# Score matmuls of two attentions issued for two heads at a time, PSUM rings of four and four, another step order

## What is computed

```python
x = x + tanh(g_xattn[0]) * _L0_xattn_ref(ctx_2048, _layernorm(x), mask, mask, ...)
x = x + tanh(g_ffn[0])   * _L0_ffn_ref(_layernorm(x), ...)
x = x + tanh(g_xattn[1]) * _L1_xattn_ref(_layernorm(x), ctx_2048, ...)
x = x + tanh(g_ffn[1])   * _L1_ffn_ref(_layernorm(x), ...)
# _L0_xattn_ref: 8 heads of 16; softmax(q k / 4, masked keys -inf) v, then W_out on [tgt, update]
# _L0_ffn_ref: dist = softmax(mean(x @ Wr + br)); idx = sorted top 4 of 16 heads, per batch
#              softmax(Qs Ks / 8) Vs for these heads, then Wo
# _L1_ffn_ref: top 2 of 8 experts per token: silu(xs w1 + b1) w2 + b2, times (xs w3 + b3); plus shared
```

## Time and profile before

| | us |
|---|---|
| median of 3 runs | 243.12 |
| lowest, highest | 242.54, 247.97 |
| span of the profiled execution | 242.8 |

### The profile page before, as it was taken

How to read it: one execution, slowest core, us unless ns; L and a number is a source line. 1 busy time by engine, 2 the same in 40 slices (tenths; PEclk the granted TensorE clock), 3 DMA queues, 4 the chain that set the end, 5 groups by cost and what they waited for, 6 DMA issues and landing times.

```text
span 242.8 us, 3827 instructions
## 1 busy us (share of the span) xinstructions
PE 211.0 (87%) x1154; PEld 152.9 (63%) x1154; DVE 151.1 (62%) x464; ACT 104.6 (43%) x283; POOL 54.0 (22%) x95
## 2 busy tenths in 40 slices
...
PEclk9995555955797999996599999999999999999999
...
DMA packets 17139, 12.45 MB, mean 51 GB/s; under 512 B 9024, under 2 KB 16416, under 8 KB 16992
## 3 DMA queue, kind: packets, MB, share of 16 engines
...
## 4 chain that ended last, share of the span: by engine, by line
PE 52%; DVE 1%; issue 1%; ACT 0%; ACTq 0%; DVEq 0%
PE dve_bank L655 7%; PE act_bank L647 7%; PE act_bank L648 6%; PE act_bank L650 4%; PE act_bank L594 3%; PE dve_bank L584 3%; PE act_bank L576 3%; PE dve_bank L640 2%; PE dve_bank L615 2%; PE dve_bank L669 2%; PE act_bank L660 2%; PE act_bank L449 2%; PE act_bank L561 1%; PE act_bank L512 1%; PE dve_bank L660 1%; PE dve_bank L612 1%
## 5 line engine op out<-in xcount | busy, mean ns | idle before, releaser
L769 ACT ACTIVATE hx<-act_bank,we 128x256 f32<-128x256 f32 x32 | 15.2, 475 | 36.1 <-PE act_bank L650 36.1
L1065 POOL TENSOR_TENSOR ctok<-ctok,cT 128x256 f32<-128x256 f32 x28 | 20.4, 729 | 44.6 <-DVE cT L994 43.5
L913 DVE TENSOR_REDUCE mx<-dve_bank 128x2 f32<-128x512 f32 x32 | 20.7, 686 | 10.4 <-PE dve_bank L496 10.3
L725 ACT ACTIVATE pT<-act_bank 128x512 f32<-128x512 f32 x32 | 17.6, 596 | 15.1 <-PE act_bank L512 14.9
L994 DVE SCALAR_TENSOR_TENSOR cT<-dve_bank,we,hx 128x256 f32<-128x256 f32 x32 | 15.0, 482 | 10.8 <-PE dve_bank L655 10.8
L1021 POOL TENSOR_SCALAR veps<-mv 128x2 f32<-128x2 f32 x16 | 3.1, 191 | 83.9 <-DVE mv L849 83.7
L647 PE MATMUL act_bank<-xw,we 128*128 128x256 f32 x64 | 20.3, 399 | 0.0
L655 PE MATMUL dve_bank<-hx,we 128*128 128x256 f32 x64 | 19.5, 404 | 0.2 <-ACT hx L770 0.2
L987 DVE TENSOR_TENSOR xw<-xnT,dve_bank 128x512 f32<-128x512 f32 x16 | 10.9, 684 | 13.3 <-PE dve_bank L640 13.3
L648 PE MATMUL act_bank<-xw,we 128*128 128x256 f32 x64 | 19.0, 379 | 0.0
L496 PE MATMUL dve_bank<-kstack,qstack 49*128 49x256 f32 x64 | 14.9, 368 | 4.5 <-DMA qstack<-parts 4.5
...
## 6 DMA issues: line engine op xcount, KB each, us to landing
we<-pack_e ACTq DMA_DIRECT2D x1, 1932.0 KB, 11.2
...
```

What stands on the lines that cost most here:

```text
L725: act.activation(pT1[:, i].rearrange("p c t -> p (c t)"), bank[:], ACT.Exp, scale=HD1 ** -0.5).then_inc(act_done, 1)
L769: act.activation(hx[:, k % EXPERT_BUFS, 0, :], bank[:, 0:T], ACT.Silu, bias=X("b1")[:, i:i + 1])
L913: dve.tensor_reduce(mx[:, b, :, i], bank[:].rearrange("p (t s) -> p t s", t=TT), AX.X, ALU.max).then_inc(dve_done, 1)
L1065: ins = pool.tensor_tensor(yT[:, b % 2, :], yT[:, b % 2, :], prod[:, k % EXPERT_BUFS, :], ALU.add)
```

## The change

Three things change together. (1) `s1`, `st1` and `s2` handle two heads per step, one in the lower and one in the upper 64 rows, with their matmuls alternating; the step takes two banks. So 64 steps of attention 1 become 32 and 16 steps of `s2` become 8; the number of matmuls and of instructions on VectorE and ScalarE stays. (2) The rings have four and four banks. (3) `ORDER` is another list. Besides, waits are written out that make reuse of `xnT`, `q2`, `k2`, `v2`, `pT2`, `pick` and the stacks wait for the last reader. In each of them the awaited step stands earlier in the new list than the waiting one.

```diff
-ACT_RING, DVE_RING = 3, 5
+ACT_RING, DVE_RING = 4, 4
-    "s1": (0, 1), "max1": (1, 0), "st1": (1, 0), ... "s2": (1, 0),
+    "s1": (0, 2), "max1": (1, 0), "st1": (2, 0), ... "s2": (2, 0),
 ORDER = """
-stat:0.0 kv:0.0 norm:0.0 stat:1.0 q:0.0 gates:0.0 kv:1.0 norm:1.0 plan_a:0.0 s1:0.0 s1:0.1 s1:0.2 s1:0.3 q:1.0
-s1:0.4 s1:0.5 s1:0.6 s1:0.7 max1:0.0 stat:2.0 stat:3.0 plan_b:0.0 plan_c:0.0 s1:1.0 s1:1.1 st1:0.0 plan_c:1.0
-st1:0.1 s1:1.2 st1:0.2 st1:0.3 s1:1.3 st1:0.4 st1:0.5 s1:1.4 s1:1.5 st1:0.6 s1:1.6 st1:0.7 s1:1.7 u:0.0 pv1:0.0
-pv1:0.1 max1:1.0 heads1:0.0 kv:2.0 depool:0.0 o1:0.0 st1:1.0 y1:0.0 st1:1.1 norm:2.0 stat:0.1 st1:1.2 st1:1.3
-q:2.0 depool:1.0 st1:1.4 st1:1.5 norm:0.1 st1:1.6 st1:1.7 consts:0.0 pv1:1.0 route:0.0 depool:2.0 pv1:1.1
-heads1:1.0 s1:2.0 s1:2.1 o1:1.0 s1:2.2 kv:3.0 y1:1.0 norm:3.0 stat:1.1 s1:2.3 q:3.0 qkv2:0.0 s1:2.4 s1:2.5
-s1:2.6 norm:1.1 s1:2.7 depool:3.0 route:1.0 max1:2.0 s2:0.0 s2:0.1 s2:0.2 scale2:0.0 s2:0.3 scale2:0.1
-scale2:0.2 pt2:0.0 st1:2.0 st1:2.1 pt2:0.1 pt2:0.2 st1:2.2 st1:2.3 scale2:0.3 st1:2.4 s1:3.0 pv2:0.0 st1:2.5
-pt2:0.3 st1:2.6 st1:2.7 s1:3.1 pv1:2.0 pv1:2.1 pv2:0.1 heads1:2.0 s1:3.2 y2:0.0 o1:2.0 stat:0.2 s1:3.3 s1:3.4
-s1:3.5 qkv2:1.0 s1:3.6 s1:3.7 y1:2.0 max1:3.0 norm:0.2 stat:2.1 s2:1.0 s2:1.1 s2:1.2 scale2:1.0 scale2:1.1
-s2:1.3 pt2:1.0 pt2:1.1 scale2:1.2 st1:3.0 y3:0.0 st1:3.1 st1:3.2 pv2:1.0 norm:2.1 stat:0.3 scale2:1.3 pt2:1.2
-st1:3.3 st1:3.4 route:2.0 pt2:1.3 st1:3.5 st1:3.6 st1:3.7 pv1:3.0 norm:0.3 pv2:1.1 gate:0.0 shared:0.0 y2:1.0
-pv1:3.1 gate_t:0.0 wide:0.0 heads1:3.0 wide:0.1 plan_c:2.0 up:0.0 up:0.1 o1:3.0 stat:1.2 up:0.2 wide:0.2 y1:3.0
-qkv2:2.0 stat:3.1 down:0.0 down:0.1 down:0.2 norm:3.1 up:0.3 norm:1.2 route:3.0 s2:2.0 wide:0.3 down:0.3 s2:2.1
...
+stat:0.0 norm:0.0 stat:1.0 gates:0.0 kv:0.0 q:0.0 norm:1.0 kv:1.0 s1:0.0 s1:0.1 s1:0.2 s1:0.3 q:1.0 stat:2.0
+max1:0.0 plan_a:0.0 st1:0.0 s1:1.0 st1:0.1 s1:1.1 plan_b:0.0 s1:1.2 s1:1.3 consts:0.0 u:0.0 st1:0.2 st1:0.3
+max1:1.0 pv1:0.0 pv1:0.1 heads1:0.0 kv:2.0 o1:0.0 st1:1.0 plan_c:0.0 st1:1.1 y1:0.0 st1:1.2 norm:2.0 stat:0.1
+stat:3.0 st1:1.3 q:2.0 pv1:1.0 pv1:1.1 norm:0.1 heads1:1.0 route:0.0 kv:3.0 s1:2.0 o1:1.0 depool:0.0
+depool:1.0 y1:1.0 s1:2.1 s1:2.2 qkv2:0.0 norm:3.0 stat:1.1 s1:2.3 s2:0.0 q:3.0 scale2:0.0 max1:2.0 s2:0.1
+norm:1.1 scale2:0.1 scale2:0.2 pt2:0.0 scale2:0.3 st1:2.0 pt2:0.1 st1:2.1 pt2:0.2 pt2:0.3 st1:2.2 route:1.0
+pv2:0.0 s1:3.0 st1:2.3 s1:3.1 pv2:0.1 pv1:2.0 y2:0.0 s1:3.2 pv1:2.1 stat:0.2 s1:3.3 qkv2:1.0 max1:3.0 norm:0.2
+s2:1.0 heads1:2.0 y3:0.0 o1:2.0 scale2:1.0 stat:0.3 st1:3.0 pt2:1.0 st1:3.1 scale2:1.1 y1:2.0 st1:3.2 stat:2.1
+s2:1.1 pt2:1.1 norm:2.1 st1:3.3 pv2:1.0 scale2:1.2 norm:0.3 scale2:1.3 route:2.0 pt2:1.2 pv1:3.0 pt2:1.3
+pv1:3.1 gate:0.0 plan_c:1.0 pv2:1.1 shared:0.0 y2:1.0 heads1:3.0 gate_t:0.0 depool:2.0 stat:1.2 wide:0.0
...
                 elif what == "s1":
-                    bank = take_dve(nd)
-                    lo, hi = 64 * j, 64 * j + ROW_MAX
-                    for t in range(TT):
-                        mm = pe.matmul(bank[:, t * T:(t + 1) * T], qstack[lo:hi, b % 2, pair, t * P:(t + 1) * P],
-                                       kstack[lo:hi, b % 2, pair, :], start=True, stop=True)
-                    mm.then_inc(dve_full, 1)
+                    banks = [take_dve(nd), take_dve(nd + 1)]
+                    for t in range(TT):
+                        for j in range(2):
+                            lo, hi = 64 * j, 64 * j + ROW_MAX
+                            mm = pe.matmul(banks[j][:, t * T:(t + 1) * T], qstack[lo:hi, b % 2, i, t * P:(t + 1) * P],
+                                           kstack[lo:hi, b % 2, i, :], start=True, stop=True)
+                            if t == TT - 1:
+                                mm.then_inc(dve_full, 1)
...
                 elif what == "norm":
+                    if b >= 2:
+                        if i == 0:
+                            act.wait_ge(dve_full, DVE_AT[("y1", b - 2, 0)] + 1)
...
                 elif what == "s1":
-                    dve.tensor_reduce(mx[:, b, :, i], bank[:].rearrange("p (t s) -> p t s", t=TT), AX.X, ALU.max
-                                      ).then_inc(dve_done, 1)
+                    for j in range(2):
+                        dve.wait_ge(dve_full, n + j + 1)
+                        dve.tensor_reduce(mx[:, b, :, PAIRS * j + i], dbank(n + j)[:].rearrange("p (t s) -> p t s", t=TT),
+                                          AX.X, ALU.max).then_inc(dve_done, 1)
```

More of the change, by code:

```diff
@@ L58 @@
     "stat": (0, 0), "norm": (1, 0),
-    "s1": (0, 1), "max1": (1, 0), "st1": (1, 0), "pv1": (1, 0), "heads1": (0, 1), "o1": (1, 0), "y1": (0, 1),
-    "route": (0, 1), "qkv2": (3, 0), "s2": (1, 0), "scale2": (0, 0), "pt2": (0, 1), "pv2": (1, 0), "y2": (0, 1),
+    "s1": (0, 2), "max1": (1, 0), "st1": (2, 0), "pv1": (1, 0), "heads1": (0, 1), "o1": (1, 0), "y1": (0, 1),
+    "route": (0, 1), "qkv2": (3, 0), "s2": (2, 0), "scale2": (0, 0), "pt2": (0, 1), "pv2": (1, 0), "y2": (0, 1),
     "y3": (0, 1),
@@ L84 @@
-pt2:2.2 down:0.4 pt2:2.3 up:0.7 pv2:2.0 norm:1.3 pv2:2.1 gate:1.0 qkv2:3.0 down:0.5 y2:2.0 down:0.6 plan_c:3.0
-down:0.7 gate_t:1.0 s2:3.0 stat:2.2 s2:3.1 wide:1.0 s2:3.2 wide:1.1 s2:3.3 scale2:3.0 y4:0.0 up:1.0 up:1.1
-norm:2.2 scale2:3.1 scale2:3.2 wide:1.2 scale2:3.3 pt2:3.0 pt2:3.1 pt2:3.2 down:1.0 up:1.2 y3:2.0 down:1.1
-stat:2.3 pt2:3.3 up:1.3 down:1.2 pv2:3.0 up:1.4 norm:2.3 wide:1.3 pv2:3.1 gate:2.0 up:1.5 down:1.3 down:1.4
-up:1.6 y2:3.0 stat:3.2 shared:1.0 gate_t:2.0 up:1.7 wide:2.0 down:1.5 down:1.6 wide:2.1 down:1.7 up:2.0 up:2.1
@@ L89 @@
-norm:3.2 down:2.0 wide:2.2 y4:1.0 y3:3.0 up:2.2 stat:3.3 down:2.1 up:2.3 up:2.4 norm:3.3 wide:2.3 down:2.2
-up:2.5 gate:3.0 down:2.3 shared:2.0 down:2.4 up:2.6 shared:3.0 down:2.5 gate_t:3.0 up:2.7 wide:3.0 down:2.6
-wide:3.1 down:2.7 up:3.0 up:3.1 up:3.2 wide:3.2 down:3.0 down:3.1 down:3.2 up:3.3 wide:3.3 up:3.4 up:3.5
-down:3.3 down:3.4 up:3.6 down:3.5 up:3.7 down:3.6 down:3.7 y4:2.0 y4:3.0
+stat:0.0 norm:0.0 stat:1.0 gates:0.0 kv:0.0 q:0.0 norm:1.0 kv:1.0 s1:0.0 s1:0.1 s1:0.2 s1:0.3 q:1.0 stat:2.0
@@ new lines @@
+pv2:0.0 s1:3.0 st1:2.3 s1:3.1 pv2:0.1 pv1:2.0 y2:0.0 s1:3.2 pv1:2.1 stat:0.2 s1:3.3 qkv2:1.0 max1:3.0 norm:0.2
+s2:1.0 heads1:2.0 y3:0.0 o1:2.0 scale2:1.0 stat:0.3 st1:3.0 pt2:1.0 st1:3.1 scale2:1.1 y1:2.0 st1:3.2 stat:2.1
+s2:1.1 pt2:1.1 norm:2.1 st1:3.3 pv2:1.0 scale2:1.2 norm:0.3 scale2:1.3 route:2.0 pt2:1.2 pv1:3.0 pt2:1.3
+pv1:3.1 gate:0.0 plan_c:1.0 pv2:1.1 shared:0.0 y2:1.0 heads1:3.0 gate_t:0.0 depool:2.0 stat:1.2 wide:0.0
+plan_c:2.0 qkv2:2.0 o1:3.0 up:0.0 norm:1.2 s2:2.0 y1:3.0 down:0.0 stat:3.1 wide:0.1 y3:1.0 up:0.1 up:0.2
@@ new lines @@
+scale2:2.0 up:0.3 norm:3.1 scale2:2.1 stat:1.3 wide:0.2 s2:2.1 wide:0.3 pt2:2.0 down:0.1 down:0.2 up:0.4
+pt2:2.1 route:3.0 up:0.5 down:0.3 pv2:2.0 up:0.6 norm:1.3 scale2:2.2 scale2:2.3 down:0.4 pt2:2.2 down:0.5
+pt2:2.3 up:0.7 gate:1.0 plan_c:3.0 pv2:2.1 down:0.6 qkv2:3.0 y2:2.0 gate_t:1.0 down:0.7 s2:3.0 wide:1.0
+stat:2.2 wide:1.1 depool:3.0 y4:0.0 up:1.0 up:1.1 norm:2.2 scale2:3.0 scale2:3.1 up:1.2 wide:1.2 down:1.0
+pt2:3.0 s2:3.1 y3:2.0 down:1.1 up:1.3 stat:2.3 wide:1.3 down:1.2 up:1.4 up:1.5 norm:2.3 scale2:3.2 scale2:3.3
```

102 lines of the change are left out of this document (71 added, 31 removed).

## The result

| | before | after |
|---|---|---|
| median, us | 243.67 (4 runs) | 252.57 (4 runs) |
| lowest, highest | 242.54, 247.97 | 251.80, 253.69 |
| span of the profiled execution | 242.8 | 251.2 |

The ratio of after to before is 1.036, with a 95% interval of 1.030 to 1.043: slower by 3.6%. The forecast was 241, with a range of 234 to 249; the time lies above the range. Medians here are over all runs of a kernel, and the ratios leave disturbed runs out, so the two can differ by some tenths of a per cent.

The account below looks back on a forecast made before the run. TensorE was taken to bound the kernel from 130.5 us on, with DMA waits and clock ahead of it. `qkv2:2.0` at 133.2, plus 102.1, plus 4.2, less 1.4, plus 2.9 gave 241 us; range 234 to 249.

Parts of the forecast that it names:

- What bounds it: TensorE bounds the half from `wide:0.0` (130.5 us) on; from 20 to 130, DMA waits and a lower clock leave holes.
- Part 1, the pairs: In `s1`, `st1` and `s2` a pair costs what one head costs, freeing 13.4 us of TensorE's time, 10 ahead of 112.
- Part 2, the rings: PSUM rings of four and four: worth nothing, at most 5.6 us if starts are uncovered; written-out waits 0, at most 2.
- Part 3, the start: `stat:1.0` ahead of `kv:0.0` makes `s1:0.0` 4.0 us late, `s1:1.0` 5.7 us late and `qkv2:0.0` 1.1 us late.
- Part 4, the middle: `route:1.0` ends at 92.9; stands of about 4 us before `qkv2:1.0` and 2.5 before `qkv2:2.0`, which starts at 133.2.
- rival B: Head fetches are covered, so the stands before `qkv2:1.0` and `qkv2:2.0` vanish: 234.5 us; chance 0.33.
- Part 5, the end: From `qkv2:2.0` on, 4.2 us more work left in the list, less 1.4 of a gap: end at 241.0 us.
- C: The late start is carried through, nothing made good by `qkv2:0.0` (later than 78.7): 248.5 us, slower; chance 0.20.
- A: The forecast itself: time freed by pairs is taken by DMA stands at both ends of the middle, 241 us; chance 0.44.
- D: The two heads of a pair don't overlap, so 13.4 us less is freed: 246 us; chance 0.03.

Follow-up runs that it names:

- e2: The changed kernel with one step moved in the list, `q:1.0` ahead of `s1:0.0` instead of behind `s1:0.3`: 245.8 us, ratio 1.006.
- e4: The changed kernel with the matmuls inside each pair in the old order, one head after the other: 252.39 us, ratio to before 1.035.
- e6: The changed kernel's code with the list of the kernel before, each pair at the place of its even head: 236.48 us, ratio 0.974.
- e9: The kernel of e6 measured once more in more rounds: 236.65 us, ratio to before 0.977.
- e5: The kernel before with PSUM rings of four and four and nothing else changed: 242.75 us, ratio 0.994.
- e12: e9 with the rings of three and five of the kernel before: 253.55 us, ratio to before 1.046.
- e11: e9 with `we` loaded behind the maxima of batch 1 and the feature loads of batches 2 and 3 behind batch 1's stacks: 239.56 us, ratio 0.986.
- e8: e7 with the load of `we` moved behind the maxima of batch 1: 238.62 us, ratio to before 0.988.
- e3: The changed kernel with the first eight steps in the order of before and `q:1.0` ahead of `s1:0.0`: 242.66 us, no interval obtained.
- e7: e3 with `stat:1.1`, `norm:1.1`, `route:1.0` ahead of `qkv2:0.0`, and `qkv2` and `s2` of batches 2 and 3 later: 240.24 us, ratio to before 0.986.
- e1: The changed kernel with the load of `we` issued behind the maxima of batch 1 instead of batch 0: 249.55 us, ratio to before 1.023.

## Why the prediction was wrong, by its steps

**What bounds it.** Right. From 130.5 to 250 TensorE is still busy for 96% (114.89 of 119.5 us), and ahead of it DMAs and clock decide.

**Part 1, the pairs.** The size was right: 13.4 us of TensorE's time, measured 15.3 (211.0 less 195.7; busy time also hangs on the clock, and e2, with the same instructions, has 191.2), and a pair costs what one head costs (0.79 us at the lower clock, 0.50 at the upper one). Taking the 2.20 us of the earlier trace rows over the rule of program order was right too, and e4 is the stronger evidence. What I made of it was half right. I took the gain ahead of 112 as "room for other steps, not time". Under the list of before the pairs bring `qkv2:0.0` from 73.8 to 70.1 (e6) and 69.0 (e9), and `wide:0.0` from 130.5 to 124.0 and 126.5. So 4 to 6.5 us of it are time, and 1 to 2.3 come in the half that TensorE bounds (104.2 and 102.9 us from `qkv2:2.0` to the end, 105.2 before), where I had 1.7.

**Part 2, the rings.** "Nothing" held for single heads (e5) and for the rings that were built. But the term was priced as if four and four were a detail, with 5.6 us as its bound. e12 shows that the pairs depend on it: with three banks for ScalarE and five for VectorE, pairs cost 10.6 us instead of gaining 6.3.

**Part 3, the start: the step that failed.** Every time up to the last issue was right within 0.5 us: VectorE's wait for the input of batch 1 (until 10.97), the parts of k (13.11), `s1:0.0` (24.28), the parts of q (31.16 to 35.39). The failed term is the last one, "3.83 us of issuing and 2.04 bring `s1:1.0` to 37.5". The 2.04 us came from a stack that had the DMA engines nearly to itself, and I carried it to a moment when 3.2 MB were in flight. It measured 9.05. I had walked only SyncE's queue and left out ScalarE's, whose loads hang on `max1:0.0`, a step that moved the other way relative to `q:1.0`. Seven us of the ten are this term.

The runs put the delay in order by how many of the six parts are issued after `ctok` (worked out by spacing the six evenly), and at three parts by whether `we` is in flight. Where none follows, other work ran or the wait was short, so 2.0 us is the most that the landing took:

| kernel | parts issued, us | `ctok` at | parts after it | `s1:1.0` after the last issue |
|---|---|---|---|---|
| before | 25.91 to 29.74 | 30.55 | 0 | 2.05 |
| e2 | 29.82 to 33.65 | 33.16 | 0 | 2.0 |
| e11 | 26.34 to 30.40 | 31.84 | 0 | 2.0 |
| e8, without `we` | 26.19 to 30.02 | 29.54 | 0 | 2.0 |
| e3 | 26.57 to 30.68 | 29.62 | 1 | 5.3 |
| e7 | 26.39 to 30.37 | 29.29 | 1 | 6.0 |
| e1, without `we` | 31.10 to 35.27 | 32.81 | 3 | 6.4 |
| after | 31.16 to 35.39 | 32.87 | 3 | 9.05 |

The DMA page of e7 for 31 to 37 us, after its six parts were issued, has the packets of just one part still to come:

```profile
q1 hardware_dynamic: 80, 0.07, 3.8%
```

What isn't shown is how the engines choose between the queues. The Trainium skill (DMA: Bandwidth & Descriptors, "Queues, rings and completion order") says that each engine takes turns between its queues, a packet at a time. If the packets of the profile are meant, SyncE's 240 packets in 36 to 44 would have passed beside as many of ScalarE's (0.67 MB), and at 320 GB/s the stack would have landed 2.7 us after 36; it landed 8.4 us after. By the rows the heavy queue got 94% and the light one 11%. Whether a packet of the rule is one of the profile no run here tells.

**Part 4, the middle.** Right in its differences. From `s1:1.0` to the third routing every step is late by 5.5 to 7.3 us, which is the offset of the start. The stand before `qkv2:1.0` was predicted at about 4 us and is 4.12, ended by a DMA of head weights; batch 1's routing ends 15.2 us later than in the earlier trace rows, which less the 6.3 us of offset is 8.9, and 8.6 were predicted. Wrong was the stand before `qkv2:2.0`: 2.5 us predicted, 0.31 seen, because `wide:0.0`, 7.0 us after the routing by my walk, came 8.8 us after it. The work ahead of it filled the wait. And the price of these stands was too high: I gave rival B 6.5 us for both, while taking all head waits away (e7 against e3) was worth 2.4.

**Part 5, the end.** From `qkv2:2.0` to the end 111.0 us, predicted 107.8. The 3.2 us are the second mis-sized term. The windows of this stretch, in e2 (the same list behind its start) and in the changed kernel, and a row of the waits of the changed kernel from 138 us on, which e2 has too:

```profile
131.07:240.40 109.33, 103.67 (x552) 76.40 (x551) 67.29 (x212) 60.33 (x152) 31.01 (x50) 1.00 0.04 9
140.18:251.20 111.02, 105.35 (x551) 77.53 (x551) 67.23 (x211) 60.43 (x152) 31.06 (x50) 0.98 0.04 9
...
PE act_bank L563 <- DMA b2h<-head_bias: 1.5, 1, 1.5
```

At the full clock TensorE's work is 103.67 us. The changed kernel has 1.7 us more, at a mean clock of 0.98. The other 1.5 us are as long as a stand at `qkv2:3.0` for its head weights; before has no such stand, and the forecast had none either. In e3 the stretch takes 110.6 us with the same 103.67 of work, so another 1.2 us of idle time can come in. The four more table loads of ScalarE lie here too, but in the changed kernel TensorE waits for ScalarE only 0.3 us in all.

**The rivals.** C's sign came: `qkv2:0.0` stood at 80.4, later than 78.7. Its mechanism came only in part. It had nothing made good between `s1:1.0` and `qkv2:0.0`, but beside before `s1:1.0` was late by 12.6 us and `qkv2:0.0` by 6.6, so 6.0 were made good, more than the 4.6 of the forecast. It was the same 2.04 us, mis-sized in C as in A, that put the time near C's. B did not happen. A's stand at `qkv2:1.0` happened, on top of the late start. D is refuted by 0.79 us.

**The sum, again.** The medians let the 16 us between the changed kernel (252.6) and the same code under the old list (236.7) be split: 6.8 for `q:1.0` behind the loads (e2), 3.1 for the first eight steps (e3), 2.4 for the head fetches (e7), and 3.6 between e7 and e9. The times of one kernel spread by 1 to 7 us. The intervals of the ratios lie apart between the changed kernel and e2, and between e2 and e7; they don't decide on the 3.1 and the 2.4 singly, nor on the last part. The traces show where the last part lies: e8, with the list of e7, reaches `qkv2:2.0` ahead of e9 (128.4 and 133.6) and loses that lead behind it, with nearly the same number of matmuls left. The windows of e8, and then of e9:

```profile
128.38:236.80 108.42, 100.82 (x514) 73.68 (x513) 62.41 (x197) 58.88 (x148) 27.41 (x43) 0.97 0.04 10
```

```profile
133.56:236.50 102.94, 98.35 (x518) 71.61 (x516) 63.86 (x205) 52.05 (x139) 29.66 (x47) 1.00 0.04 10
```

So the end of the new list costs 5.5 us more than that of the old one, 2.5 of it in busy time at a clock of 0.97 and 3.0 in idle time. No run took this end apart.
